# Adding the experts' rows back: from TensorE with diagonal weights to ScalarE, GpSimd and VectorE

## The reference

```python
x = x + _L1_ffn_ref(_layernorm(x, axis=-1), L1_ffn_w_router, L1_ffn_w_gate, L1_ffn_w_down)
# in it, N = 2048 tokens, 8 experts, 2 chosen for each token:
hidden = silu(xf @ w_gate.T)
combine = (topk_gates[:, :, None] * one_hot(topk_idx, 8)).sum(axis=1)
y = zeros((N, D))
for e in range(8):
    y = y + combine[:, e:e + 1] * (hidden @ w_down[e].T)
...
x = x + _L2_xattn_ref(_layernorm(x, axis=-1), ctx_1024, ctx_1024, ...)
```

## Time and profile before

| | |
|---|---|
| median of three runs | 1609.93 us |
| the profiled execution | 1609.93 us |
| its span | 1608.0 us |
| PE busy in the span | 1375.8 us (86%) |
| DVE busy | 1031.2 us (64%) |
| ACT busy | 762.5 us (47%) |
| POOL busy | 503.1 us (31%) |
| the block `shared_hidden_experts` | from about 967.6 to 1050.8 us |
| the block `experts_return` with statistics | from 1050.8 to about 1072.2 us |

### The profile page before, as it was taken

The page is one execution under the profiler, slowest core; times in us unless marked ns, Lnnn a source line. Parts: engine busy times, 40 slices in busy tenths (PEclk is TensorE's granted clock), DMA queues, the critical chain, the costliest instruction groups (busy, mean ns, idle before and its releaser), DMA issues. The chain is left out here.

```text
span 1608.0 us, 29727 instructions
## 1 busy us (share of the span) xinstructions
PE 1375.8 (86%) x9356; PEld 1078.5 (67%) x9357; DVE 1031.2 (64%) x2764; ACT 762.5 (47%) x1811; POOL 503.1 (31%) x536
## 2 busy tenths in 40 slices
PE   4976999999999999999998696979845589739993
PEld 3754777877887778777876465757623257639993
DVE  3455776777677777777774754458878869662223
ACT  1304565556555655566565233127657456313331
POOL 3232222222222323232321206525621224325551
PEclk9988999999999999999999798899977589969997
DMA  8000000000000100000001444252010000101124
GB/s 312 20 1 1 2 1 1 0 1 0 0 27 1 36 1 0 0 0 0 0 1 38 176 196 144 83 209 119 1 40 1 3 3 1 53 23 67 66 65 168
DMA packets 29275, 74.92 MB, mean 47 GB/s; under 512 B 7799, under 2 KB 13192, under 8 KB 27388
## 3 DMA queue, kind: packets, MB, share of 16 engines
q1 hardware_dynamic: 22364, 55.63, 9.3%
q0 software_dynamic: 6816, 18.14, 3.5%
HBM read 54.41 MB, written 20.88 MB: 47 GB/s over the span
## 5 line engine op out<-in xcount | busy, mean ns | idle before, releaser
L1085 PE MATMUL banks<-l_ffn_in_wqkv,l_ffn_hT 128*128 128x512 f32 x384 | 180.4, 606 | 0.9 <-ACT l_ffn_hT L1249 0.9
L1168 PE MATMUL banks<-l_ffn_h2T,l_ffn_in_w 128*128 128x128 f32 x1408 | 175.7, 277 | 0.0
L1168 PEld LDWEIGHTS banks<-l_ffn_h2T,l_ffn_in_w 128*128 128x128 f32 x1408 | 167.0, 192 | 7.3 <-issue 5.7
L1271 ACT ACTIVATE l_ffn_work<-l_ffn_work,l_ffn_att_bias 128x256 f32<-128x256 f32 x256 | 126.4, 495 | 70.9 <-DVE l_ffn_att_bias L1423 70.9
L1300 ACT ACTIVATE l_ffn_gate<-banks,l_ffn_layer_cols 128x128 f32<-128x128 f32 x160 | 51.7, 364 | 183.5 <-PE banks L1168 170.3
L1085 PEld LDWEIGHTS banks<-l_ffn_in_wqkv,l_ffn_hT 128*128 128x128 f32 x384 | 68.8, 192 | 74.5 <-issue 73.4
L1034 POOL TENSOR_TENSOR l_ffn_rden_wide<-l_ffn_att_rden,ones 128x512 f32<-128x512 f32 x32 | 33.2, 1039 | 252.8 <-DVE l_ffn_att_rden L1434 252.8
L1176 PE MATMUL banks<-l_ffn_in_w,l_ffn_ff 128*128 128x256 f32 (+1 forms) x384 | 104.5, 388 | 0.0
L2927 POOL TENSOR_TENSOR L__probs<-L__probs,L__rec 128x1024 f32<-128x1024 f32 x32 | 60.8, 1901 | 101.9 <-DVE L__rec L2887 101.9
L1308 ACT ACT_TABLE_LOAD x68 | 87.2, 1283 | 1.2
L1039 POOL TENSOR_TENSOR l_ffn_rstd<-l_ffn_ve,neg_half 128x1 f32<-128x1 f32 x32 | 20.3, 633 | 206.7 <-DVE l_ffn_ve L1460 206.7
(11 more groups left out here) (446 smaller groups left out, 3350.2 us busy)
## 6 DMA issues: line engine op xcount, KB each, us to landing
l_plan_rows<-l_plan_pairs SPq DMA_DIRECT2D x16, 512.0 KB, 7.7
l_ffn_in_w<-in_L_w SPq DMA_DIRECT2D x2, 4096.0 KB, 17.5
l_ffn_in_down<-in_L_down SPq DMA_DIRECT2D x1, 4096.0 KB, 13.2
l_plan_pairs<-l_plan_rows SPq DMA_DIRECT2D x4, 1024.0 KB, 7.0
l_plan_table<-l_plan_rows SPq DMA_DIRECT2D x8, 512.0 KB, 2.7
l_ffn_in_wqkv<-in_L_wqkv SPq DMA_DIRECT2D x1, 3072.0 KB, 12.1
l_ffn_in_w<-in_L_w SPq DMA_DIRECT2D x4, 640.0 KB, 12.2
x_res<-in_x SPq DMA_DIRECT2D x4, 512.0 KB, 5.1
```

What stands on the lines that cost most here:

```text
L1085: mm = pe.matmul(ps[:, (Q, K, V)[n], :], hT[:, m.b, m.odd, ch, 1 - ch:P + 1 - ch], wqkv[:, bass.ds(m.layer, 1), ch, n * INNER:(n + 1) * IN ...
L1168: mm = pe.matmul(ps[:, HIDDEN[pair], to:to + P], w1[:, ch, at:at + P], h2T[:, ch, m.b, :], start=(j % 2, n, ch) == (0, 0, 0), stop=ch == D ...
L1271: ex = nc.scalar.activation(work[:, m.b, slot, :], work[:, m.b, slot, :], ACT.Exp, bias=bias[:, m.b, slot:slot + 1], scale=-1.0, accum_out ...
```

## The change

PE no longer takes part in `experts_return`. The diagonal matrices and the eight DVE instructions that wrote them go, and with them 3 + 32 matmuls of PE, three copies of ACT and five additions of DVE from PSUM. In their place, for each tile `t`:

- ACT multiplies the rows of the first choice by their gates, in place in SBUF, one instruction for each batch entry (`ACT.Copy` with a column as scale), and signals `gate_ready`;
- POOL adds this product to `x`, one instruction over both batch entries (`first_choice`), and signals `bias_added`;
- DVE multiplies the rows of the second choice by their gates and adds them to `x`, one instruction for each batch entry, and then takes the statistics as before.

All of these read and write SBUF only. The DMAs, the use without statistics and everything else keep their order.

```diff
-                if t in DIAGONAL_AT:
-                    at = DIAGONAL_AT.index(t) * OF_ONE
-                    own = slice(at, at + OF_ONE)
-                    v.tensor_tensor(diag[:, own, :], e.ident[:].unsqueeze(1).broadcast_to((P, OF_ONE, P)),
-                                    plan.weights[:, own].unsqueeze(2).broadcast_to((P, OF_ONE, P)), ALU.mult)
...
         @block.gpsimd
         def _(p):
+            def first_choice(t):
+                p.wait_ge(s.gate_ready.sem, s.gate_ready.at(t))
+                x = by_batch(e.x[:])[:, :, t, :]
+                p.tensor_tensor(x, of_choice(t, 0), x, ALU.add).then_inc(s.bias_added.sem, 1)
...
             if with_stats:
                 pool.begin(p)
-                for g in range(TILES // 2):
-                    rstd(g)
-
-        @block.tensor
-        def _(pe):
-            def old_rows(t):
-                pe.matmul(ps[t], e.ident[:], by_batch(e.x[:])[:, :, t, :], start=True, stop=False, skip_group_check=True)
-
-            def gated(t):
-                pe.wait_ge(returned[t], 16)
...
+                first_choice(0)
                 for t in range(TILES):
-                    gated(t)
+                    if t + 1 < TILES:
+                        first_choice(t + 1)
+                    if t % 2:
+                        rstd(t // 2)
 
         @block.scalar
         def _(act_):
             if with_stats:
-                for t in range(BY_PE):
-                    act_.wait_ge(s.out_psum.sem, s.out_psum.at(t))
-                    nc.scalar.copy(by_batch(e.x[:])[:, :, t, :], ps[t].rearrange("p (b d) -> p b d", b=BATCH)).then_inc(s.x_done.sem, 1)
+                for t in range(TILES):
+                    act_.wait_ge(returned[t], 16)
+                    for b in range(BATCH):
+                        i = (t + b * TILES) * CHOICES
+                        gated = nc.scalar.activation(back[:, i, :], back[:, i, :], ACT.Copy, scale=plan.weights[:, i:i + 1])
+                    gated.then_inc(s.gate_ready.sem, 1)
...
+            for t in range(TILES):
                 v.wait_ge(returned[t], 16)
-                for c in range(CHOICES):
+                if with_stats:
+                    v.wait_ge(s.bias_added.sem, s.bias_added.at(t))
+                for c in range(1 if with_stats else 0, CHOICES):
                     for b in range(BATCH):
                         i = (t + b * TILES) * CHOICES + c
                         add = v.scalar_tensor_tensor(tile_of(e.x, t, b), back[:, i, :], plan.weights[:, i:i + 1], tile_of(e.x, t, b), ALU.mult, ALU.add)
```

More of the change, by code:

```diff
@@ L2187, in take, with shared_hidden_experts @@
         cp.then_inc(s.up_w_ready.sem, 1)
[L2190 removed]
+def shared_hidden_experts(e, ctx, stage, plan, w_down, quantiser):
     nc, s, ps = e.nc, e.s, e.ps
@@ L2440, in own_experts, with experts_return @@
     end(turns, *three)
-def experts_return(e, stage, plan, back, diag=None):
-    nc, s, ps = e.nc, e.s, e.ps
+def experts_return(e, stage, plan, back, with_stats):
+    nc, s = e.nc, e.s
     dve, pool = e.chain["dve"], e.chain["pool"]
-    with_stats, BY_PE = diag is not None, 3
     returned = [e.dma_sem(f"{stage}_returned{t}") for t in range(TILES)]
@@ L2450, in experts_return @@
     if with_stats:
-        begin(1, s.ln_var, s.ln_rstd, s.out_psum)
+        begin(1, s.ln_var, s.ln_rstd, s.gate_ready, s.bias_added)
     by_batch = lambda a: a.rearrange("p (b t) d -> p b t d", b=BATCH)
+    of_choice = lambda t, c: back.rearrange("p (b t c) d -> p b t c d", b=BATCH, c=CHOICES)[:, :, t, c, :]
     with nc.Block(no_gpsimd_drain=True) as block:
@@ L2535, in add_back @@
                 add.then_inc(s.x_done.sem, 1)
[L2537 to L2543, removed]
+                if with_stats:
+                    v.wait_ge(s.x_done.sem, s.x_done.at(t))
+                    for b in range(BATCH):
+                        bn = v.bn_stats(e.bn[:, b, :], tile_of(e.x, t, b))
+                    dve.link(bn)
+                    for b in range(BATCH):
+                        mv = v.bn_aggr(e.mean_var[:, t + b * TILES, :], e.bn[:, b, :])
+                    mv.then_inc(s.ln_var.sem, 1)
     end(TILES, s.x_done)
     if with_stats:
-        end(TILES, s.ln_var, s.out_psum)
+        end(TILES, s.ln_var, s.gate_ready, s.bias_added)
         end(TILES // 2, s.ln_rstd)
@@ L2561, in l1_ffn @@
             route(e, early, "l1_route", given, plan, DROPPING_TILES, w_gate)
-        diag = memory(e, ctx, "l1_return")("diag", [P, ITEMS, P])
         with ExitStack() as early:
-            shared_hidden_experts(e, early, "l1_experts", plan, w_down, Quantiser(e, early, ffn, raw), diag)
+            shared_hidden_experts(e, early, "l1_experts", plan, w_down, Quantiser(e, early, ffn, raw))
         back = plan.rows[:, 0:ITEMS // 2, :].rearrange("p t (a d) -> p (t a) d", d=D)
-        experts_return(e, "l1_experts", plan, back, diag)
+        experts_return(e, "l1_experts", plan, back, True)
 PARTS = 3
@@ L3271, in l3_ffn @@
                         lambda x, f: w2[:, bass.ds(x, 1), f, :].rearrange("p x n -> p (x n)"))
-        experts_return(e, "l3_experts", plan, plan.rows[:, 0:ITEMS, :])
+        experts_return(e, "l3_experts", plan, plan.rows[:, 0:ITEMS, :], False)
 def rotary():
```

9 lines of the change are left out of this document (removed).

## The result

| | before | after |
|---|---|---|
| median of five runs each, same chip (us) | 1609.77 | 1618.42 |
| profiled execution of after (us), span | | 1622.5, 1620.4 |
| return block: first DMA issued to `less_mean` (us) | 22.28 | 29.89 |
| `less_mean` to the attention's first scores (us) | 4.63 | 6.28 |

The ratio is 1.0064, 95% interval 1.0037 to 1.0092: slower, by 8.7 us by the medians and 10.3 us by the ratio. The forecast was 1619.7 us, range 1612.5 to 1624.0. The profiled execution of after was already 5.0 us late when POOL issued the experts' first gather, in code that the change does not touch. So I compare stretches, not spans. The two stretches of the table add up to 26.91 us before and 36.17 after, +9.26. The "first scores" are PE's first product of the queries with the keys.

A forecast was written before the change was run, and what follows sets the result against it. From tile 2 on, engines rather than DMA arrival bound the return block, with its last `rstd` on the kernel's path. 1609.93 + 7.8 (return block) + 2.0 (PE's clock) = 1619.7 us, range 1612.5 to 1624.0.

The forecast's parts named there:

- the start: Return block until tile 1's statistics: DVE's tile 1 waits for POOL's addition of tile 2, 2.0 us later than before.
- the turns: Return block, two tiles each, from tile 1's statistics to tile 7's: 5.85, 5.85 and 4.6 us, +5.8 in all.
- Return block: The block where the chosen experts' rows are gated and summed: +7.8 us, from 2.0 and 5.8.
- the first rival: POOL and DVE do not exclude each other: return block +4.1, 1616.0 us; chance 0.22 with what lies between.
- The clock: Start of the next block's attention: PE, idle over 30 us, begins at a lower clock, +2.0 us, bounds 0 and 4.0.
- The diagonals: Experts' block: removing the eight DVE instructions counts 0; bounds a gain of 3.7 us and a loss of 2.
- the 2 us that the prediction named as a sign against it: The step is wrong if the experts' block changes its 83.2 us by more than 2.
- Who is first: Return block: after tile 1's addition POOL takes tile 2 ahead of DVE, starting 0.04 us later against DVE's 0.03 after a semaphore.
- The second rival: Exclusion costs more than one addition a turn: return block +9 to +13 us, 1621 to 1625 us; chance 0.11.
- The third: Experts' block: fewer DVE instructions shift or remove its unexplained waits, 10 to 15 us back, about 1605 us; chance 0.05.
- the fourth in its first form: Experts' block waits shorten in part, by 7 to 13 us: within 3 us of 1609.93; chance 0.10 for both forms.
- The fourth in its second form: No exclusion, warm PE and part of POOL's 3.7 us gained: within 3 us of 1609.93; chance 0.10 for both forms.

The follow-up runs named there:

- kernel 1: The changed kernel with the second input of DVE's gate-and-add read from PSUM (constants) instead of SBUF: return block 25.67 us, ratio 1.0057.
- kernel 2: The changed kernel with POOL's additions three tiles ahead of each `rstd` instead of one: return block 26.96 us, ratio 1.0047.
- kernel 6: The changed kernel with both DVE's second input in PSUM and POOL's additions three tiles ahead: return block 22.64 us, ratio 1.0022.
- the second profile: The changed kernel once more, with no further edit: return block 29.60 us, way to the first scores 6.84 us, ratio 1.0083.
- Kernel 3: The changed kernel with ten small PE matmuls after each of the first seven tiles: return block 30.44 us, to scores 4.61 us, ratio 1.0048.
- Kernel 4: The changed kernel with the eight DVE instructions writing the diagonals put back, unread: experts' block 79.16 us, ratio 1.0059.
- kernel 7: The changed kernel with POOL's additions three tiles ahead and small matmuls keeping PE busy: return block 28.33 us, ratio 1.0038.
- kernel 8: The kernel before, with PE doing six tiles and ACT with POOL the other two: return block 20.73 us, to scores 6.29 us, ratio 1.0010.
- kernel 9: As kernel 8, with small matmuls added in PE's gaps: return block 22.63 us, to scores 5.01 us, ratio 1.0013 to the kernel before.

## Why the prediction was right

The sum forecast +9.8 us; the two stretches have +9.26, the medians +8.7. The interval of the ratio is 6 to 15 us, so that the total came within 1.3 us is not evidence for the terms. The stretches are, and there the terms partly cancel: the start was put 0.6 us too high and the turns 0.4 us too low, so the 0.2 us by which the block was missed is in part luck.

- **The start, +2.0.** From the issue to tile 1's statistics: 11.82 us, before 10.42 (1061.22 less 1050.80). So +1.4. The wait came at another place than forecast. Tile 1 was there 5.99 us after the issue, where the kernel before had it after 6.73, so its addition followed tile 0's at once and tile 0's pair waited for it (1.90 us). Tile 1's pair met only the last 0.1 us of tile 2's addition.
- **The turns, 5.85, 5.85 and 4.6.** Measured 5.88, 5.85 and 4.93: 16.66 us, +6.2 instead of +5.8. The term that was off is `rstd`: 1.63 to 1.67 us within the turns instead of 1.36. ACT's two rows took 0.91 us, not 1.1, which changes nothing, as ACT keeps up either way.
- **Return block +7.8.** Measured +7.61. Kernels 1, 2 and 6 divide it: 4.2 are the exclusion, 2.9 the place of the additions between the `rstd`s, 0.4 the three-engine chain itself. In the prediction the exclusion was the difference from the first rival, 7.8 less 4.1, so 3.7. The sum was right and had both in it, as the wait for tile 4's addition and as `rstd` at the head of each turn. My reading of it afterwards, that the exclusion was all, was wrong.
- **The clock, +2.0.** Measured +1.65, and 2.2 in the second profile. Kernel 3 shows that it is the clock. The forecast lies between the two.
- **The diagonals, 0.** Kernel 4 saw no gain. The experts' block was 0.8 us shorter than before's in the first profile of after and 2.6 us in the second, beyond the 2 us that the prediction named as a sign against it; but it moves by 4.5 us between kernels with the same instructions there (77.62 to 82.07), so that sign could decide nothing. That PE bounds this block was read and not tested.
- **Who is first.** Held in after: POOL's second addition took SBUF ahead of DVE. The Trainium skill ("SBUF — State Buffer", Who interferes with whom) says that issue order decides who blocks. Kernels 2 and 7 agree, with 1.86 against 2.85 us for the same pair.
- **Rivals.** The first, no exclusion, wanted gate-and-adds of 0.48 us beside POOL and a block of +4.1: excluded by 1.80 us, and what it would have been is kernel 1's block. The second rival's lost races appear in kernel 7 but not in after; its small additions that wait appear in after, with 0.3 us a turn instead of 0.4 to 1.3. The third, and the fourth in its first form, needed the experts' block to be 7 us shorter or more; a wait of DVE of the kind that they name, 5.72 us, is still there in after. The fourth in its second form needed a warm PE, and the key product took 2.05 us.

## What to carry to other kernels

Before work is moved from a busy engine to idle ones, look where the inputs lie. A VectorE instruction with two large SBUF inputs and a large GpSimd instruction do not run beside each other; with one of the inputs in PSUM they do. Look at the order on the helper too: an addition that DVE needs, queued behind a small operation that itself waits for DVE's statistics, cost 2.9 us here beside the contention's 4.2. And the engine that is relieved has a clock: what TensorE no longer does in one block, it may pay back at the start of the next.

## What the runs showed of the hardware

- POOL's small operations are longer beside such a DVE pair: `L2470` 0.35 us and `L2471` 1.13 to 1.17, against 0.20 and 1.02 in kernel 1, where the pair's second input lies in PSUM, and 1.02 at the block's end, where DVE has nothing. I had taken the undisturbed price.
- A wait does not cost the whole of the instruction that waits: after POOL's end at 1070.96 the pair needed only 0.69 of its usual 0.85 us.
- The granted clock can fall without a long pause: kernel 8's key product came after 2.26 us of idleness and took 1.74 us, with a granted clock of 0.61 up to the transposition; the kernel before's came after 2.36 us, took 1.13 and had 1.00. What PE did earlier in the block differs, 16.95 of 20.73 us busy against 19.44 of 22.30. That this is the cause was not isolated: kernel 9 had both fewer pauses in the block and a shorter one, 0.42 us, ahead of the key product.
- A scatter of POOL that starts while DVE writes a diagonal is longer: in the kernel before those at 1035.57, 1037.73 and 1039.90, each 0.10 us behind the start of such an instruction, took 1.45, 1.44 and 1.44 us, the ones after them 0.98.
